# Values of the previous step issued between the two score pairs of a step, in both attentions of a hybrid network on one Trainium2 core

## The reference, cut to what matters

```python
# _L0_conv_ref, for each shift and each half of the channels
qkv = jnp.einsum('bchw,oc->bohw', xsp, wq)
...
attn = jax.nn.softmax(jnp.einsum('whqc,whkc->whqk', qw, kw), axis=-1)
ow = jnp.einsum('whqk,whkc->whqc', attn, vw) + lw
# _L2_attn_ref
attn = jnp.einsum('bhqd,bhkd->bhqk', q, k)
attn = jax.nn.softmax(attn, axis=-1)
out = jnp.einsum('bhqk,bhkd->bhqd', attn, v)
return out @ w_proj + b_proj
```

## Time and profile before

| what | value |
|---|---|
| runs of the kernel before | 4033.07 us median, 4028.87 to 4033.74 |
| span of the profiled execution | 4026.0 us, first to last instruction |
| its own time | not listed apart; the runs are 3 to 8 us longer than this span |
| busy in the span | PE 85%, DVE 62%, ACT 48%, POOL 21% |
| window attention, 333 to 785 us | 452 us: PE busy 371.36, DVE 318.15, ACT 318.12, granted clock 0.82 |
| token attention, 1142 to 2512 us | 1370 us: PE busy 1250.41, DVE 1247.70, ACT 1036.59, granted clock 0.99 |

### The profile page before, as it was taken

How to read it: one execution, slowest core, us unless ns; L and a number is a source line. 1 busy time by engine, 2 the same in 40 slices (tenths; PEclk the granted TensorE clock), 3 DMA queues, 4 the chain that set the end, 5 groups by cost and what they waited for, 6 DMA issues and landing times. The chain is left out here.

```text
span 4026.0 us, 66483 instructions
## 1 busy us (share of the span) xinstructions
PE 3440.5 (85%) x24463; PEld 1530.3 (38%) x24463; DVE 2489.7 (62%) x4082; ACT 1927.2 (48%) x2321; POOL 860.5 (21%) x866
## 2 busy tenths in 40 slices
PE   6997887647599999999999998789878479999999
PEld 4664555424322222222222221633567334444444
DVE  3227767465489999998999995344486323333333
ACT  1214667512147777777777777334323223233322
POOL 0001333300000000000000000034200245555555
PEclk9997778778779999999999999789989589999999
DMA  4444555400500000000000000044101122222221
GB/s 144 125 126 103 115 118 119 88 1 2 180 18 16 21 21 21 22 20 21 15 26 21 16 21 6 17 138 150 53 0 43 33 81 85 84 87 85 84 84 47
DMA packets 137544, 247.17 MB, mean 61 GB/s; under 512 B 34808, under 2 KB 47264, under 8 KB 136800
## 3 DMA queue, kind: packets, MB, share of 16 engines
q1 hardware_dynamic: 137312, 243.98, 21.8%
HBM read 171.55 MB, written 56.62 MB: 57 GB/s over the span
## 5 line engine op out<-in xcount | busy, mean ns | idle before, releaser
L1073 DVE TENSOR_REDUCE mxv<-mx_ps 128x1 f32<-128x512 f32 x2048 | 1276.9, 683 | 88.8 <-PE mx_ps L932 70.6
L1048 ACT ACTIVATE PT<-st_ps 128x1024 f32<-128x1024 f32 x1024 | 997.1, 1022 | 297.3 <-PE st_ps L945 297.1
L932 PE MATMUL mx_ps<-KS,QS 24*128 24x512 f16 x2048 | 613.3, 394 | 114.0 <-DVE mxv L1073 96.6
L1921 DVE TENSOR_TENSOR u<-h_ps,s 128x512 f32<-128x512 f32 x352 | 243.5, 692 | 541.6 <-ACT s L1899 494.6
L959 PE MATMUL o_ps<-PT,VA 128*32 128x512 f32 x4096 | 550.0, 609 | 0.5 <-ACT PT L1048 0.5
L1951 POOL TENSOR_TENSOR hg<-u,gb 128x512 f32<-128x512 f32 x352 | 450.9, 1283 | 394.1 <-DVE u L1921 297.4
L1899 ACT ACTIVATE s<-h_ps 128x512 f32<-128x512 f32 x352 | 210.2, 597 | 587.3 <-PE h_ps L1875 587.3
L1883 PE MATMUL y_ps<-hg,m_w 128*128 128x512 f32 x704 | 361.4, 597 | 55.2 <-POOL hg L1951 55.1
L945 PE MATMUL st_ps<-QS,KS 26*128 26x512 f16 x2048 | 400.4, 387 | 9.2 <-ACT TX L1038 8.5
L667 DVE TENSOR_REDUCE mxv<-mx_ps 128x4 f32<-128x512 f32 x512 | 319.7, 683 | 118.3 <-PE mx_ps L542 113.8
L945 PEld LDWEIGHTS st_ps<-QS,KS 26*128 26x128 f16 x2048 | 96.5, 91 | 558.2 <-issue 479.7
(11 more groups left out here) (228 smaller groups left out, 4173.1 us busy)
## 6 DMA issues: line engine op xcount, KB each, us to landing
gb<-g SPq DMA_DIRECT2D x64, 512.0 KB, 3.7
gb<-g SPq DMA_DIRECT2D x16, 2048.0 KB
QK<-qk SPq DMA_DIRECT2D x128, 192.0 KB
qk<-hl SPq DMA_DIRECT2D x80, 256.0 KB, 3.3
RB<-d SPq DMA_DIRECT2D x48, 256.0 KB, 3.5
qk<-hl SPq DMA_DIRECT2D x64, 128.0 KB, 3.2
v<-vs SPq DMA_DIRECT2D x32, 256.0 KB
VS<-v SPq DMA_DIRECT2D x32, 256.0 KB, 3.1
```

The costliest lines, as they stand in the source:

```text
L932: nc.tensor.matmul(mx_ps[:, use % 3, :], rows(QS, g // 2, j, STACK)[:, t * C:(t + 1) * C], rows(KS, g // 2, j, STACK)[:, half * HALF:(half ...
L1048: nc.scalar.activation(PT[:, n % 2, 2 * a:2 * a + 2], st_ps[:, a], ACT.Exp, scale=1.0 / SHIFT ** 2).then_inc(st_free[a], 1)
L1073: nc.vector.tensor_reduce(mxv[:, g % 2, j, t, half:half + 1], mx_ps[:, slot], AX.X, ALU.max).then_inc(mx_free, 1)
```

## The change

In both attentions V of step n-1 moves from the end of step n to a place between its score pairs: after M2 and M3, ahead of the transpose if the step has one, and so ahead of pair a = 1. The fill moves from ahead of pair a = 1 to ahead of pair a = 0, and then writes the bank of that pair. No instruction is added or taken away on any engine, and the other four engines' programs stay as they are.

```diff
@@ window_attention
                 def scores(n, a):
                     u, s = n // 4, n // 2 % 2
-                    if a == 1:
+                    if a == 0:
                         fill_array(nc, st_ps[:, a, 1], ident, KS[:, u, s, 0:HALF])
...
                             if a:
                                 continue
+                            if n:
+                                values(i, n - 1)
+                            elif kind != "first":
+                                values(i - 1, STEPS - 1)
                             if n % 4 == TURN and (kind != "last" or u < 3):
...
                                     turn(use)
-                        if n:
-                            values(i, n - 1)
-                        elif kind != "first":
-                            values(i - 1, STEPS - 1)
```

More of the change, by code:

```diff
@@ L1011, in image @@
                                 continue
+                            if n:
+                                values(i, n - 1, kind)
+                            elif kind != "first":
+                                values(i - 1, STEPS - 1, "mid")
                             if n % KT == TURN and (kind != "last" or g < G - 1):
@@ L1016, in image @@
                                 turn(use)
[L1017 to L1020, removed]
                 periods(pe, image)
```

## The result

The changed kernel takes 4069.15 us (median of four runs, 4066.62 to 4077.04) against 4033.4 us for the kernel before in the runs beside it: a ratio of 1.0094, 95% interval 1.0081 to 1.0107, so some 38 us slower. The profiled execution took 4066.62 us, with a span of 4064.8 us against 4026.0, +38.8.

A forecast was written before the change was run, and what follows sets the result against it. It took tokens to be bound by the slot ring with VectorE nearly full, windows by the chain transpose, copy, SyncE, DMA, scores. Tokens +20 and windows +39 us gave +59, from 4033 to 4092 us, range 4050 to 4150.

The forecast's parts named there:

- The slot ring: Tokens: the wait cycle through the three slots, now M0, M3, V, M0, keeps its length of 2.53 us a step.
- a new ring through E1: Tokens: E1, release of TensorE, V and the S pair up to its exponential form a cycle of 2.56 us a step.
- The transpose costs 0.15 us behind V: Tokens: placed behind V, the transpose costs only TensorE's 0.15 us instead of 0.63, a gain of 0.48 us a group.
- The copy in the ring: Tokens, group's end: ScalarE's copy follows E1 and the next group's first V waits for it, 0.48 us more.
- A group 21.11 us: Tokens: a group goes from 20.87 to 21.11 us, +0.24, over 62 groups with maxima +15 us.
- The projection's step: Tokens, seven images: the projection begins behind M1 and costs 2.59 us over an ordinary step instead of 3.19, -4 us.
- quiet step 3.09: Windows: V waits for the copy behind E1, so a step takes 3.09 us against 2.58 wherever the rows' chain doesn't bind.
- 13 half images: Windows: the leg from scores to transpose has two V instead of one, +2.2 us each, +29 us in all.
- this leg stays SyncE's: Windows, transpose to scores: TensorE's own work would take about 20 us, under 23.58, so SyncE still sets the leg.
- the windows absorb it: Rival, windows: the rows' DMA lands earlier relative to the transpose and half images keep their length, 4063 us; chance 0.15.
- The clock's rival: Rival, windows: the clock falls in ordinary steps too, making the ring 4.19 us and the kernel 4159 us; chance 0.10.
- The faster case: Rival: the transposes' lost time comes back and nothing replaces it, 30 us off, 4003 us; chance 0.06.

The follow-up runs named there:

- e1: Both edits of the change made in the window attention only, tokens as in the kernel before: 4052.53 us, ratio 1.0051 to the kernel before.
- e5: The full change with ScalarE's copy of o_ps between a step's two exponentials instead of behind them, in both attentions: 4055.39 us, ratio 1.0051 to the kernel before.
- e4: The full change with the fill left ahead of pair a = 1 in both attentions: 4232.99 us, ratio 1.0504 to the kernel before.
- e2: Both edits of the change made in the token attention only, windows as in the kernel before: 4046.57 us, ratio 1.0046 to the kernel before.
- e6: The kernel before with V early only in the token steps that have a transpose: 4023.65 us, ratio 0.9983 to the kernel before.
- e9: The kernel before with V early only at token transposes, and the windows' denominator write ahead of SyncE's regrouping loads: 4000.76 us, ratio 0.9921.
- e10: The kernel before with early V at token transposes, earlier denominator write, and a second fill in the token step after each transpose: 3997.22 us, ratio 0.9904.

## Why the prediction was right, and which terms were not

The direction and the reasons held: 4069 us against 4092 predicted, inside 4050 to 4150. The forecast had +59 us and the span grew by 38.8: the tokens came out as forecast, in part by luck, and the windows at +25.2 instead of +39. e1 alone has 1.0051 [1.0033, 1.0069], some 13 to 28 us, so the forecast for the windows was too high by more than that interval allows.

- **The slot ring stays 2.53, a new ring through E1 is closed, 2.56.** Right; it is 2.60. The release of TensorE by ScalarE is 0.15 us, not the 0.05 that I took from the scores after the projection. Nearer would have been a row in which V itself waits. S1 to E1 is 0.43 instead of 0.49.
- **The transpose costs 0.15 us behind V.** It costs nothing that shows: S1 starts 2.60 us after the last one in that step too.
- **The copy in the ring, +0.48.** +0.43, and e5 takes most of it out by moving the copy alone.
- **A group 21.11 us, +0.24.** 21.17 to 21.21, mean +0.32, because of the release: 62 x 0.32 = +20 us instead of +15. The projection's step costs 2.54 us over an ordinary group instead of 3.19 before (predicted 2.59 against 3.19), -0.65 x 7 = -5 us instead of -4. One term was missing: the trace of before has one fall of the clock in the tokens behind a projection (one group of 24.06 took 26.82 us and the next 22.42 instead of 20.87, 4.3 us together), e1, with the same tokens, has it in the same groups, and the changed order has none. With about +8 us at the end (predicted +9) these make 20 - 5 - 4 + 8 = 19 against the 17.7 measured, and 20 predicted. That the two agree is partly luck: the release that was put too low and the fall of the clock that was left out cancel.
- **Windows, quiet step 3.09.** 3.10. That it doesn't set the half images is shown by e4 and e5, where quiet steps of 3.41 and 2.76 us leave them at 30.43 and 30.58. For the first and last image 25.2 - 13 x 1.44 = 6.5 us remain instead of 10, but this can't be told from chance: what lies outside the 13 half images is 68 to 79 us in the three profiles with the window order of before.
- **13 half images, +2.2 each, +29 us.** This is the step that was mis-sized: +1.44, +19 us (one profile of each order; e1 has 30.69, e2 and e6 with the order of before 28.87 and 29.88). Two parts of it failed. "At half clock", with both V at 1.94 us, was the upper end, and the first V does take 1.94; but the second takes 1.08 at a clock that is back, so the leg from the stop is 6.29 instead of 7.3 in this half image and +1.99 in the mean. And "this leg stays SyncE's" was taken as a fixed length from the transpose: SyncE issued the rows 0.9 us sooner after the transpose, since VectorE's copy of the turned maxima came 0.5 us sooner behind V and SyncE waited less for the next transpose; 0.3 us of it went into the time from issue to scores, and the leg lost 0.55 us. The rows issued at 393.17 in the earlier trace rows are not those of the transpose at 379.16 but of the next unit's at 390.05; what ties the two is SyncE's queue, and that is why the leg could move.
- **The rivals.** That the windows absorb it gave 4063 us, nearer to the result than the forecast, but not for its reason: it had half images of unchanged length, and they grew by 1.44 us; of what the second V added, 0.55 of 1.99 was absorbed. The clock's rival is false: with V waiting 0.44 us in each quiet window step and TensorE busy 5.83 of 7.00 us, the granted clock is 1.00. The Trainium skill, in "TensorE: Matmul & The Clock Gate", section "A second HAM failure mode: psum-queue depth-cycling", has frequent short gaps between groups of matmuls make the clock fall and rise; this trace does not show it in quiet steps. The faster case failed where the prediction put its deciding point: the new ring is 2.60 us, over the 2.45 that it would have needed.

## What to carry to other kernels

Moving a consumer between two producers closes a ring: add up producer, release, consumer and next producer, and look at what already shares that stretch (here a copy on ScalarE and a fill; the fill alone would have cost 0.32 us in each of 512 steps). Where an engine waits for a DMA, shorter steps on that engine can give nothing (e5 in the windows): look in the queue that issues the DMA for a wait that stands ahead of it, which here was worth 0.6% with one move. Where two edits are tied together in one change, run each half and each stage by itself, and a result that is near for the wrong reason becomes visible.

## What was not expected of the hardware

- ScalarE releases TensorE for V 0.14 to 0.15 us after its own end in the records (423.56 to 423.70 in the windows, 1635.29 to 1635.44 in the tokens), against 0.05 us for the score pair after the bias. In the tokens V's fp32 weights are loaded in between, from 1635.41. That the loading makes the difference was not tried.
- In e6 the granted clock fell to 0.50 although TensorE was busy 5.58 of the 6.40 us ahead of it, with score and maxima matmuls but no values in some 3.2 us before the next V. There are five such falls in e6 and six in e9; with one more fill in that stretch (e10) there is none. What of the work decides it was not settled.
